# Grouped attention of a two-layer transformer step: from batch loops to one unrolled order of units with the side work between them

## Chip, cores and metric

The kernel runs on one core of one Trainium2 chip. The metric is the device time of one execution in microseconds (us), the median of several runs.

## What is computed

The inputs are 4 batches of 256 tokens with 256 features. The reference runs a cross attention with fp8 rounding, a ternary feed-forward part, a second cross attention with int8-quantised weights, and then the last layer, in which the change lies: an RMS norm, projections to 32 query heads and 8 key and value heads of 64 features, rotary parts on queries and keys, causal grouped attention (four query heads share one key head), an output projection of 2048 by 256 added to the residual stream, and a mixture of 16 experts with the four best per token. Cut to the attention of the last layer:

```python
q, k = _rope(q, k)                      # q*cos + rot(q)*sin, the same for k
# 4 query heads share a key and value head, causal
p = softmax(q @ k.T / sqrt(64) + mask)  # per batch and head, 256 x 256
x = x + (p @ v).reshape(4, 256, 2048) @ wo
```

## The kernel before, in words

Everything is one program on one core with explicit semaphores. Each engine runs its own list of instructions in the order in which the program writes them. The stages follow one another: the cross attentions and the feed-forward part (to about 338 us of the trace), the grouped attention (to about 676 us), then routing and experts. Only the grouped attention differs between the two kernels, and the names below belong to it.

**Precision.** Queries and keys are kept as two float16 halves, hi and lo. `products` multiplies hi by hi, hi by lo and lo by hi and sums in PSUM. A projection piece is 128 tokens by 512 columns: six matmuls. A batch has twelve pieces, six per block `t` of 128 tokens: the keys (`c` = 0), four pieces of queries (`c` = 1 to 4, eight heads each) and the values (`c` = 5).

**Side work of a piece** (keys and queries). TensorE projects it (`project`, products at L1648). VectorE multiplies by cosine and sine (L1323, L1324, L1326) and adds the two parts (L1330) in `rope`. ScalarE makes the hi half (`token_hi`, L885 for queries, L887 for keys; L879 is the copy of the values). GpSimd makes the lo half (`token_lo`, L696 and L698). Then TensorE turns the piece by eight transposes (`turn_tokens`, L1815), and VectorE (L1348) or ScalarE (L895) copies the turned heads from PSUM to `qt`, `kat` or `kbt`.

**Units.** A unit is one key head with its four query heads and one block of 128 queries. A batch has 16 units, alternately with 128 keys (`t` = 0) and 256 keys (`t` = 1). The chain of a unit is: scores (`a_score`, L1791 to L1793, the middle one adds the causal mask), the negated row maximum on VectorE (`score_max`, L1338), four exponentials with their sums on ScalarE (L922), reciprocal on VectorE (L1364), normalisation on GpSimd (L706), transposes on TensorE (`a_turn`, L1832), copies to `apt` by VectorE (L1360) and, for 256 keys, ScalarE (`pt_second`, L902), products with the values (`a_values`, L1847), and the hi (`output_hi`, L907) and lo (L1369) halves of the result in `ot_hi` and `ot_lo`.

**Order.** In `attend` a loop step `i` issues on TensorE the scores of unit `i`, the transposes of unit `i - 3` and the value products of unit `i - 4`. After the 16 units of a batch come the output projection (96 products of 128 by 256 in two groups, L1648), the addition to `xn` (L1382) with its statistics, and the remaining pieces of the next batch: four projections stand in steps 16 and 17, two in step 19, the other six around the output projection, the twelve turns behind them. The first three batches are one hardware loop (`Fori(0, B - 1)`) on each of the four engines, the last batch stands behind it in straight code. `turn_bank` gives each turn its PSUM bank. Scores use banks 0 to 3, transposes 4 and 5, value products 6 and 7. SyncE loads expert weights; some loads wait for the last projection (`proj`) and some for the last addition (`x4_added`). Behind the attention VectorE adds `xn` to `x`, six of eight blocks of it (L1379) ahead of the last output projection's additions.

The lines that set the order of TensorE in a batch:

```python
for i in range(AU + 4):
    if 1 <= i < AU:
        a_score(b, i)
    if 3 <= i < AU + 3:
        a_turn(i - 3)
    if i >= 4:
        a_values(i - 4)
```

## Time and profile before

| What | Value |
|---|---|
| Median of 3 runs | 863.56 us (863.39 to 863.63) |
| Profiled execution, its own time | 863.33 us |
| Its span in the trace | 861.5 us |
| Mean granted clock of TensorE, share of full | 0.9 |
| Instructions in the trace | 17134 |
| TensorE (PE) busy | 634.3 us, 74% of the span |
| VectorE (DVE) busy | 616.5 us, 72% |
| ScalarE (ACT) busy | 441.7 us, 51% |
| GpSimd (POOL) busy | 445.0 us, 52% |

How to read it: a span is the time from the first to the last instruction of the trace. The busy shares are means over stages that have different limits, so the attention is read by itself. PE is TensorE's matmuls, PEld its weight loads, which run beside them; a matmul's duration holds its passage through the array, so that neighbours overlap and the distance of starts tells the pace. Timeline rows start with the time of the first instruction and the time until the last one ends; a bracket at the end names idle time and what ended it.

### The profile page before, as it was taken

How to read it: one execution, taken by the hardware profiler on the slowest of the kernel's cores; microseconds unless marked ns; L12 is line 12 of the kernel's file. 1: busy time of each engine (PE TensorE's matmuls, PEld its weight loads, DVE VectorE, ACT ScalarE, POOL GpSimd, SP SyncE). 2: the span in 40 equal slices, each digit the busy share in tenths (PEclk: the TensorE clock that was granted, in tenths of full speed). 3: DMA queues.
4: the chain of work that ended last, by engine and by line, in shares of the span. 5: the costliest groups of instructions: out<-in, count | busy, mean ns of one | idle time of the engine just before them, and what ended most of it. 6: DMA issues, size and time to landing. Idle time of an engine off the chain costs nothing.

```text
span 861.5 us, 17134 instructions
## 1 busy us (share of the span) xinstructions
PE 634.3 (74%) x5889; PEld 462.7 (54%) x5889; DVE 616.5 (72%) x1476; ACT 441.7 (51%) x1230; POOL 445.0 (52%) x397
## 2 busy tenths in 40 slices
PE   0214997277878754589988998899798638999980
PEld 0102666255646542378666866776587515666650
DVE  5998758787887787958786777678776393555544
ACT  4712633176857711368336824773486206767650
POOL 1463763189999903435334532553264216777760
PEclk9998998698989967889999999999999758999995
DMA  9400130327656502000000000000300543333437
GB/s 291 160 1 0 50 99 21 102 75 221 206 182 198 184 37 110 1 2 2 2 1 0 0 0 0 0 0 0 146 2 2 222 160 91 108 104 107 108 88 250
DMA packets 39896, 71.73 MB, mean 83 GB/s; under 512 B 5024, under 2 KB 31392, under 8 KB 39328
## 3 DMA queue, kind: packets, MB, share of 16 engines
q1 hardware_dynamic: 35232, 58.03, 20.1%
q0 software_dynamic: 4608, 12.98, 5.1%
q8 instruction: 32, 0.52, 0.3%
q14 instruction: 24, 0.20, 0.1%
HBM read 49.96 MB, written 21.04 MB: 82 GB/s over the span
## 4 chain that ended last, share of the span: by engine, by line
PE 28%; POOL 25%; issue 23%; DVE 16%; DMA 3%; ACT 3%; SPq 1%; POOLq 0%; DVEq 0%; ACTq 0%
POOL arena L706 8%; PE ps L1940 8%; PE ps L1963 4%; PE ps L1648 3%; PE ps L1615 2%; POOL arena L661 2%; POOL arena L657 2%; PE ps L1575 2%; POOL arena L696 2%; PE ps L1593 2%; POOL work L696 2%; DVE xn L1007 1%; PE ps L1917 1%; PE ps L1847 1%; PE ps L1952 1%
## 5 line engine op out<-in xcount | busy, mean ns | idle before, releaser
L706 POOL TENSOR_TENSOR arena<-arena,tiny 128x512 f32<-128x512 f32 x64 | 93.9, 1467 | 99.1 <-DVE tiny L1364 99.1
L922 ACT ACTIVATE arena<-ps,tiny 128x128 f32<-128x128 f32 (+1 forms) x256 | 104.9, 436 | 33.4 <-DVE tiny L1338 33.4
L1338 DVE TENSOR_REDUCE tiny<-ps 128x4 f32<-128x512 f32 x64 | 61.1, 954 | 35.9 <-PE ps L1793 35.5
L1940 PE MATMUL ps<-arena 128*128 (+1 forms) x288 | 72.4, 389 | 0.8 <-issue 0.3
L1791 PE MATMUL ps<-arena 128*128 128x128 f16 (+1 forms) x256 | 61.5, 258 | 14.9 <-ACT arena L922 10.5
L1648 PE MATMUL ps<-arena,xt_hi 128*128 128x512 f16 (+1 forms) x224 | 64.4, 372 | 3.6 <-DVE xt_lo L1137 3.0
L728 POOL DMA_INDIRECT arena<-h_store,arena x48 | 47.0, 980 | 33.6 <-DVE arena L1477 19.3
L1491 DVE SCALAR_TENSOR_TENSOR ps<-ps,arena 128x256 f32<-128x256 f32 x48 | 20.8, 433 | 57.6 <-ACT arena L972 57.6
L1360 DVE COPY arena<-ps 128x512 f32<-128x512 f32 x64 | 44.0, 687 | 23.9 <-PE ps L1832 23.9
L1793 PE MATMUL ps<-arena 128*128 128x128 f16 (+1 forms) x256 | 60.4, 255 | 0.0
L734 POOL DMA_INDIRECT y_store<-arena x48 | 47.4, 988 | 21.4 <-issue 12.2
L1847 PE MATMUL ps<-arena 128*64 128x128 f32 x768 | 56.1, 281 | 2.5 <-DVE arena L1369 2.5
L1832 PE MATMUL ps<-ident,arena 128*128 128x128 f32 x384 | 54.2, 278 | 4.7 <-DVE arena L1360 2.4
L922 ACT ACTIVATION_READ_ACCUMULATOR arena<-ps,tiny 128x1 f32 x256 | 56.5, 221 | 0.0
L835 ACT ACTIVATE arena<-arena 128x256 f32<-128x256 f32 x128 | 54.6, 507 | 2.8 <-DVE arena L1250 2.6
L1792 PE MATMUL ps<-causal,ident_bf 128*128 128x128 bf16 x256 | 53.4, 227 | 0.0
L1832 PEld LDWEIGHTS ps<-ident,arena 128*128 128x128 f32 x384 | 44.0, 144 | 7.7 <-issue 6.0
L1847 PEld LDWEIGHTS ps<-arena 128*64 128x64 f32 x768 | 40.7, 136 | 13.4 <-issue 10.0
L1250 DVE CUSTOM_DVE_ANT_0 arena<-ps,arena 128x256 f32<-128x256 f32 x128 | 46.7, 420 | 0.0
L1575 PE MATMUL ps<-ident,work 128*128 128x128 f32 x64 | 14.6, 423 | 42.3 <-DVE work L1032 26.0
L1705 PE MATMUL ps<-ident,arena 128*128 128x128 f32 x256 | 36.8, 290 | 11.0 <-issue 3.3
L1648 PE MATMUL ps<-arena 128*128 128x256 f16 x384 | 43.1, 273 | 0.9 <-DVE arena L1369 0.9
(298 smaller groups left out, 1851.5 us busy)
## 6 DMA issues: line engine op xcount, KB each, us to landing
e_store<-arena SPq DMA_DIRECT2D x16, 768.0 KB, 4.3
arena<-e_store SPq DMA_DIRECT2D x16, 768.0 KB, 7.3
xn<-w_dram SPq DMA_DIRECT2D x24, 256.0 KB, 4.6
work<-w_dram SPq DMA_DIRECT2D x24, 256.0 KB, 4.7
arena<-w_gate_up_t_dram SPq DMA_DIRECT2D x2, 1024.0 KB, 9.0
arena<-wq_dram SPq DMA_DIRECT2D x2, 1024.0 KB, 7.5
arena<-wo_dram SPq DMA_DIRECT2D x2, 1024.0 KB, 5.4
work<-y_store SPq DMA_DIRECT2D x4, 512.0 KB, 6.5
```

Source lines behind the costliest of these rows:

```text
L706: nc.gpsimd.tensor_tensor(p, p, arec[:, u % 4, :].unsqueeze(2).broadcast_to([P, GH, L]), ALU.mult)\
L734: nc.gpsimd.indirect_dma_start(y_store, bass.IndirectOffsetOnAxis(index[:, i:i + 1], 0), y[:, i % YBUF, :], None).then_inc(y_sent[i % YBUF ...
L835: nc.scalar.activation(xp[:, i % 2, h, :], masked[:, i % 2, h, :], ACT.Exp, bias=xnm[:, i % 4, h:h + 1], scale=-1.0).then_inc(x_exp, 1)
L922: nc.scalar.activation(ap_[i % 3][:, h, 0:L], ps[:, (i % 2) * 2 + h // 2, (h % 2) * S:(h % 2) * S + L], ACT.Exp, bias=anm[:, i % 4, h:h + ...
L1338: nc.vector.tensor_reduce(anm[:, i % 4, :].rearrange("p (m h) -> p m h", m=2), scores, AX.X, ALU.max, negate=True).then_inc(a_max, 1)
L1648: last = mm(dst, l, r, start=(n == 0), stop=(n == 3 * len(pairs) - 1))
L1791: mm(ps[:, bank, at:at + L], q, kat[:, g, 0:L], start=True, stop=False)
L1792: mm(ps[:, bank, at + t * P:at + L], ident_bf[:, :], causal[:, :], start=False, stop=False)
L1793: last = mm(ps[:, bank, at:at + L], q, kbt[:, g, 0:L], start=False, stop=True)
L1832: last = nc.tensor.transpose(ps[:, 4 + k, h * P:(h + 1) * P], ap_[u % 3][:, h, k * P:(k + 1) * P], ident[:, :])
L1847: last = mm(ps[half * HD:(half + 1) * HD, 6 + u % 2, pair * P:(pair + 1) * P], av[:, k, g * HD:(g + 1) * HD], apt[:, u % 2, k, h * P:(h + ...
L1940: last = mm(ps[:, 2 + i % 2, :], xg[:, i % 2, x_half * KB + k, :], weights(hidden_weights(slot, w_half, k), i), start=(n == 0), stop=(n == 5))
```

## The change

The three hardware loops and the last batch's body become one unrolled loop over all 64 units (`UNITS`) on every engine, and two tables drive the side work:

- `SIDE` lists the 48 projection pieces with the unit behind which each is issued. Eight pieces of batch 0 stand in front (-1); in each batch the four query pieces of `c` = 3 and 4 of its own stand at units 0, 1, 2 and 4, and eight pieces of the next batch at units 5, 6, 8, 9, 10, 12, 13 and 14. Behind the start every piece uses PSUM bank 7.
- `TURNS` lists the 48 turns with the unit, bank and copying engine: behind the start always bank 4, ScalarE at odd units, VectorE at even ones.
- A step `i` on TensorE issues the transposes of unit `i - 2` (before `i - 3`), the scores of unit `i`, a turn and a projection where the tables have one (turn first at even units), the value products of unit `i - 2` (before `i - 4`), and six products of the output projection for unit `i - 3`. The output projection thus accumulates in bank 6 over the 16 units; both additions to `xn` and both statistics of a batch run in one go, in step 3 of the next batch.
- Scores with 128 keys use bank 0, with 256 keys banks 1 and 2. The transposes use banks 3 and 4; the value products have bank 5 alone and wait until the unit before has been read.
- The add of the rotary part moves from VectorE to GpSimd (`rope_sum`) for all pieces behind the start; there it precedes the normalisation, and the lo half follows it.
- `kat`, `kbt` and `av` are doubled (one for each parity of the batch); the halves of queries wait in a ring of four pieces (`q2`, `QRING`), the output halves in a ring of four units.
- The large addition `x + xn` runs in step 64, ahead of the last unit's copy. SyncE's list is unchanged.

The core of the diff (removed bodies and sizes of tiles are left out):

```diff
+UNITS = B * AU
+KEY, VAL = 0, 5
+def in_place_order():
+    first = [(KEY, 0), (KEY, 1), (1, 0), (1, 1), (VAL, 0), (VAL, 1), (2, 0), (2, 1)]
+    order = [(0, c, t, -1) for c, t in first]
+    own = [(3, 0), (3, 1), (4, 0), (4, 1)]
+    following = [(KEY, 0), (KEY, 1), (VAL, 0), (VAL, 1), (1, 0), (1, 1), (2, 0), (2, 1)]
+    at = [0, 1, 2, 4, 5, 6, 8, 9, 10, 12, 13, 14]
+    for b in range(B):
+        groups = [(b, c, t) for c, t in own] + [(b + 1, c, t) for c, t in following if b + 1 < B]
+        order += [g + (b * AU + u,) for g, u in zip(groups, at)]
+    return order
+SIDE_BANK = [(7, 6, 5, 2, 1, 0, 7, 6)[n] if n < 8 else 7 for n in range(len(SIDE))]
+def turns_in_order():
+    order = [(0, 0, -1, 4, "act"), (0, 1, -1, 3, "vec"), (1, 0, -1, 4, "act"), (1, 1, -1, 3, "vec"),
+             (2, 0, -1, 4, "act"), (3, 0, -1, 3, "vec")]
+    at = {(3, 0): 2, (3, 1): 3, (4, 0): 5, (4, 1): 7, (1, 0): 13, (1, 1): 14, (2, 0): 15, (2, 1): 17}
+    keys = {(0, 0): 8, (0, 1): 9, (1, 0): 10, (1, 1): 11}
...
+    return order + [(n, h, u, 4, "act" if u % 2 else "vec") for n, h, u in later]
@@ GpSimd
+            def rope_sum(n):
+                m = ROPES.index(n)
+                pool.wait_ge(rope_parts, m + 1)
+                nc.gpsimd.tensor_tensor(yb[:, m % 2, :], yb[:, m % 2, :], yr[:, m % 2, :], ALU.add).then_inc(roped, 1)
...
+            for i in range(UNITS + 1):
+                before = [n for n in sides_at(i - 1) if n in ROPES] if i else []
+                for n in before:
+                    rope_sum(n)
+                if i:
+                    normalise(i - 1)
+                for n in before:
+                    token_lo(n)
@@ ScalarE
+            for n in sides_at(-1)[:6]:
+                token_hi(n)
+            for r in turns_at(-1):
+                if TURNS[r][4] == "act":
+                    turned_tokens(r)
+            for n in sides_at(-1)[6:]:
+                token_hi(n)
+            for i in range(UNITS + 3):
+                if i >= 3:
+                    output_hi(i - 3)
+                if 2 <= i < UNITS + 2 and i % 2:
+                    pt_second(i - 2)
+                for n in sides_at(i - 1) if i else []:
+                    token_hi(n)
+                for r in turns_at(i - 1) if i else []:
+                    if TURNS[r][4] == "act":
+                        turned_tokens(r)
+                if i < UNITS:
+                    exponentials(i)
@@ VectorE
+            def add_attention(b):
+                vec.wait_ge(wo_out, (b + 1) * AU)
+                for t in range(TB):
+                    nc.vector.scalar_tensor_tensor(xn[:, b * TB + t, :], ps[:, 6, t * D:(t + 1) * D], 1.0 / WS,
+                                                   xn[:, b * TB + t, :], ALU.mult, ALU.add).then_inc(x4_added, 1)
+                vec.wait_ge(x4_added, (b + 1) * TB)
+                for t in range(TB):
+                    stat(b * TB + t, xn)
...
+            for i in range(UNITS + 3):
+                if 2 <= i < UNITS + 2:
+                    pt_first(i - 2)
+                if 1 <= i <= UNITS:
+                    row_reciprocal(i - 1)
+                if i >= 3:
+                    output_lo(i - 3)
+                if i < UNITS:
+                    score_max(i)
+                if i > AU and i % AU == 3:
+                    add_attention(i // AU - 1)
+                for r in turns_at(i):
+                    if TURNS[r][4] == "vec":
+                        turned_tokens(r)
+                for n in sides_at(i):
+                    if n in ROPES:
+                        rope(n)
+                if i == UNITS:
                     nc.vector.tensor_tensor(x[:, 0:T - TB, :], x[:, 0:T - TB, :], xn[:, 0:T - TB, :], ALU.add)
+            add_attention(B - 1)
@@ TensorE
+            def turn_tokens(r):
+                n, half, _, bank, _ = TURNS[r]
+                b, c, t, _ = SIDE[n]
+                pe.wait_ge(tok_split, ropes_to(n))
+                past = [q for q in range(r) if TURNS[q][3] == bank]
+                if past:
+                    pe.wait_ge(*read_out(past[-1]))
+                if TURNS[r][2] > 2:
+                    pe.wait_ge(a_pt2, (TURNS[r][2] - 1) // 2)
...
+            def out_projection(u):
+                b, g, t = u // AU, u % AU // TB, u % TB
+                pe.wait_ge(a_o_read, u + 1)
+                if u % AU == 0 and b:
+                    pe.wait_ge(x4_added, b * TB)
+                for o in range(2):
+                    hi, lo = ot_hi[:, u % 4, o, :], ot_lo[:, u % 4, o, :]
+                    for l, r in ((hi, wo_hi), (hi, wo_lo), (lo, wo_hi)):
...
+                        last = mm(ps[:, 6, t * D:(t + 1) * D], l, r[:, g * 2 + o, :], start=first, stop=final)
+                last.then_inc(wo_out, 1)
...
+            for n in sides_at(-1):
+                project(n)
+            pe.wait_ge(kb_zeroed, TB)
+            for r in turns_at(-1):
+                turn_tokens(r)
+            for i in range(UNITS + 3):
+                if 2 <= i < UNITS + 2:
+                    a_turn(i - 2)
+                if i < UNITS:
+                    a_score(i)
+                if i % 2 == 0:
+                    for r in turns_at(i):
+                        turn_tokens(r)
+                for n in sides_at(i):
+                    project(n)
+                if i % 2:
+                    for r in turns_at(i):
+                        turn_tokens(r)
+                if 2 <= i < UNITS + 2:
+                    a_values(i - 2)
+                if i >= 3:
+                    out_projection(i - 3)
```

## Rows read from the trace of the kernel before

**Rows 1.** Stretches: length; busy (count) of PE, PEld, DVE, ACT, POOL; PEclk; DMA.
```profile
339.57:676.26 336.69, 297.02 (x2970) 230.50 (x2968) 247.66 (x464) 188.89 (x672) 140.13 (x104) 0.95 0.03 10
...
371.26:453.43 82.17, 74.69 (x748) 58.04 (x746) 61.01 (x117) 47.02 (x168) 35.05 (x26) 0.96 0.01 1
384.95:404.59 19.64, 19.64 (x242) 16.61 (x241) 15.98 (x32) 17.26 (x77) 11.75 (x9) 1.00 0.01 2
375.00:380.00 5.00, 2.38 (x16) 1.81 (x14) 1.58 (x4) 3.33 (x16) 2.93 (x2) 0.78 0.00 2
657.23:665.15 7.92, 5.76 (x68) 4.36 (x66) 4.03 (x10) 3.74 (x12) 2.68 (x2) 1.00 0.01 2
```

**Rows 2.** Timeline of TensorE in the middle of batch 0, by starts.
```profile
394.57 0.60 PE L1832 MATMUL ps<-ident,arena 128*128 128x128 f32 x4
...
395.10 1.09 PE L1847 MATMUL ps<-arena 128*64 128x128 f32 x16
...
396.13 0.23 PE L1791 MATMUL ps<-arena 128*128 128x128 f16 x1
...
396.81 1.04 PE L1832 MATMUL ps<-ident,arena 128*128 128x128 f32 x8
...
397.78 0.66 PE L1847 MATMUL ps<-arena 128*64 128x128 f32 x8
...
398.37 0.28 PE L1791 MATMUL ps<-arena 128*128 128x256 f16 x1
...
399.48 0.60 PE L1832 MATMUL ps<-ident,arena 128*128 128x128 f32 x4
```

**Rows 3.** Waits from batch 0 to batch 1 (371.26 to 453.43 us).
```profile
POOL arena L706 <- DVE tiny L1364: 25.4, 16, 9.5
```

**Rows 4.** Timeline: two projections, the next transposes, token turns, the output projection.
```profile
413.01 0.60 PE L1648 MATMUL ps<-arena,xt_hi 128*128 128x512 f16 x2
...
415.61 0.60 PE L1832 MATMUL ps<-ident,arena 128*128 128x128 f32 x4
...
443.89 2.84 PE L1815 MATMUL ps<-ident_h,arena 128*128 128x128 f16 x48
...
665.15 10.65 PE L1648 MATMUL ps<-arena 128*128 128x256 f16 x96 [0.94 <-DVE arena L1369]
```

**Rows 5.** Timeline of one unit with 256 keys: its maximum, right behind its scores, and its normalisation.
```profile
621.02 1.23 DVE L1338 TENSOR_REDUCE tiny<-ps 128x4 f32<-128x1024 f32 x1 [1.44 <-PE ps L1793]
...
624.51 1.89 POOL L706 TENSOR_TENSOR arena<-arena,tiny 128x1024 f32<-128x1024 f32 x1 [1.06 <-DVE tiny L1364]
```

**Rows 6.** Costs of side work: batch 1's groups; by line (min/median/max), L1330 and L1379.
```profile
L1330 DVE TENSOR_TENSOR arena<-arena 128x512 f32<-128x512 f32 x10 | 9.6, 962 | 0.3
L895 ACT ACTIVATE arena<-ps 128x1024 f16<-128x1024 f16 x5 | 5.0, 1023 | 2.9 <-PE ps L1815 2.9
L696 POOL TENSOR_TENSOR arena<-arena 128x512 f16<-128x512 f32 x4 | 4.6, 1157 | 8.1 <-ACT arena L885 8.1
L885 ACT ACTIVATE arena<-arena 128x512 f16<-128x512 f32 x4 | 2.5, 630 | 8.6 <-DVE arena L1330 8.6
...
L1330 DVE TENSOR_TENSOR arena<-arena x40: 691/1145/1575, 341.0 to 610.4; 128x512 f32<-128x512 f32 x40
...
L1379 DVE TENSOR_TENSOR x<-x,xn x1: 1748/1748/1748, 665.0 to 665.0; 128x1536 f32<-128x1536 f32 x1
```

**Rows 7.** Timeline at the start and the end of the grouped attention.
```profile
339.57 0.69 DVE L1323 TENSOR_TENSOR arena<-ps,cos 128x512 f32<-128x512 f32 x1 [1.56 <-PE ps L1648]
...
364.41 2.47 DVE L1348 COPY arena<-ps 128x1024 f16<-128x1024 f16 x4
...
369.82 0.31 PE L1791 MATMUL ps<-arena 128*128 128x128 f16 x1
...
654.99 1.23 DVE L1338 TENSOR_REDUCE tiny<-ps 128x4 f32<-128x1024 f32 x1 [0.70 <-PE ps L1793]
...
675.84 0.42 DVE L1382 SCALAR_TENSOR_TENSOR xn<-ps,xn 128x256 f32<-128x256 f32 x1 [4.35 <-PE ps L1648]
```

More of the change, by code:

```diff
@@ new lines, in exponentials @@
+            def exponentials(u):
+                L = (u % TB + 1) * P
+                act.wait_ge(a_max, u + 1)
+                if u >= 3:
+                    act.wait_ge(a_pt_trans, u - 2)
+                for h in range(GH):
+                    nc.scalar.activation(ap_[u % 3][:, h, 0:L], head_scores(u, h), ACT.Exp, bias=anm[:, u % 4, h:h + 1],
+                                         accum_out=asum[:, u % 4, h:h + 1]).then_inc(a_exp, 1)
+            for n in sides_at(-1)[:6]:
+                token_hi(n)
@@ L1392, in _, with rope_whole, turned_tokens @@
-            for n in range(10):
-                rope(0, n)
-            turned_tokens(0)
-            with vec.Fori(0, B - 1) as b:
-                attend(b, True)
-            attend(B - 1, False)
+            def rope_whole(n):
+                rope(n)
+                m = ROPES.index(n)
+                vec.wait_ge(rope_parts, m + 1)
+                nc.vector.tensor_tensor(yb[:, m % 2, :], yb[:, m % 2, :], yr[:, m % 2, :], ALU.add).then_inc(roped, 1)
+            def turned_tokens(r):
+                vec.wait_ge(tok_transposed, r + 1)
+                nc.vector.tensor_copy(turn_target(r), heads_bank(TURNS[r][3])).then_inc(qt_vec, 1)
@@ L1776, in project @@
                     w = [(wq_hi[:, k, (c - 1) * 512:c * 512], wq_lo[:, k, (c - 1) * 512:c * 512]) for k in range(KB)]
-                else:
-                    w = [(wkv_hi[:, c // 5, k, :], wkv_lo[:, c // 5, k, :]) for k in range(KB)]
-                rows = bass.ds((b * TB + t) * P, P) if not isinstance(b, int) else slice((b * TB + t) * P, (b * TB + t + 1) * P)
-                products(ps[:, c, :], [((xt_hi[:, k, rows], xt_lo[:, k, rows]), w[k]) for k in range(KB)])\
+                rows = slice((b * TB + t) * P, (b * TB + t + 1) * P)
@@ L1781, in project @@
+                products(ps[:, SIDE_BANK[n], :], [((xt_hi[:, k, rows], xt_lo[:, k, rows]), w[k]) for k in range(KB)])\
                     .then_inc(proj, 1)
-            def a_score(b, u):
-                n, g, t = b * AU + u, u // TB, u % TB
+            def turn_tokens(r):
+                n, half, _, bank, _ = TURNS[r]
+                b, c, t, _ = SIDE[n]
+                pe.wait_ge(tok_split, ropes_to(n))
[4 more added lines that the diff above has]
+                    pe.wait_ge(a_pt2, (TURNS[r][2] - 1) // 2)
+                for h in range(8):
+                    src = (kb2 if half else ka)[t][:, h, :, :] if c == KEY else half_heads(n)[:, h, :, :]
+                    last = nc.tensor.transpose(ps_h[:, bank, h * P:(h + 1) * P], src.rearrange("p m d -> p (m d)"),
+                                               ident_h[:, :])
+                last.then_inc(tok_transposed, 1)
@@ L1788, in a_score @@
                 for h in range(GH):
                     q = qt[:, g * GH + h, t * P:(t + 1) * P]
[L1790 to L1793 removed]
+                    dst = head_scores(u, h)
@@ new lines, in a_values @@
+            def a_values(u):
+                b, g, t = u // AU, u % AU // TB, u % TB
+                if g == 0:
+                    pe.wait_ge(v_ready, b * TB + t + 1)
+                pe.wait_ge(a_pt, u + 1)
+                if t:
+                    pe.wait_ge(a_pt2, u // 2 + 1)
+                if u:
+                    pe.wait_ge(a_o_read, u)
+                for pair in range(GH // 2):
+                    for k in range(t + 1):
+                        for half in range(2):
+                            h = pair * 2 + half
+                            last = mm(ps[half * HD:(half + 1) * HD, 5, pair * P:(pair + 1) * P],
+                                      av[b % 2][:, k, g * HD:(g + 1) * HD], apt[:, u % 2, k, h * P:(h + 1) * P],
+                                      start=(k == 0), stop=(k == t))
+                last.then_inc(a_o, 1)
```

426 lines of the change are left out of this document (175 added, 251 removed).

## Prediction, written before the changed kernel was run

> **What bounds the kernel now.** I read the stretches of the grouped attention first: from its first rotary part to its last addition it takes 336.7 us, with TensorE busy 297.0 [rows 1]. In the middle of a batch's units TensorE is busy 19.64 of 19.64 us [rows 1], and its timeline shows a cycle without a gap: a pair of units (one with 128 keys, one with 256) is transposes 0.53, values 1.03, scores 0.68, transposes 0.97, values 0.59, scores 1.11, together 4.91 us, and the next pair's transposes start at once [rows 2]. So there TensorE is the bound, and the change removes nothing from it. VectorE (15.98) and ScalarE (17.26 of 19.64) come close behind. But a batch takes 82.2 us, not 8 x 4.91 = 39.3 [rows 1]: 42.9 us go to the passage between batches (twelve projections, the rotary parts, twelve token turns, the output projection). The waits of that stretch name its chain: GpSimd's normalisation waits 25.4 us for reciprocals in one batch [rows 3], as no unit runs in the passage.
>
> **TensorE's work per batch**, by starts. Two projections take 415.61 - 413.01 = 2.60 us, so one 1.3; 48 token transposes are six turns in 2.84, so 0.47 each; the output projection is two times 48 products in 10.65 [rows 4]. Per batch: 39.3 + 12 x 1.3 + 12 x 0.47 + 10.65 = 71.1 us. Against 82.2 that leaves 11 us per batch to win. It is the floor of the new loop, as every product remains.
>
> **The new loop.** A step i issues transposes(i-2), scores(i), a turn and/or a projection, values(i-2), output products(i-3) (six, 0.67 us). A step without side work costs 2.9 (even) or 3.35 us (odd); a projection adds 1.3, a turn 0.47. I walked one batch, every engine in its written order.
> - Round trip of an odd unit: behind its scores the maximum starts at 621.02; exponentials and reciprocal follow, and the normalisation ends at 626.40 [rows 5]: 5.4 us, 5.5 from the scores to the transposes. With side work in the following even step there are at least 5.9 us of TensorE work between, so it is hidden. Odd steps always have such a neighbour in the first three batches.
> - VectorE: the add of the rotary part (mean 0.96 us [rows 6]) leaves it. Per step it has 2.0 us of unit work on average (15.98 in eight steps [rows 1]), 1.5 of the three multiplications (2.48 per rope now, below, less the add) and in an even step at times a 0.7 copy: some 4.2, where TensorE needs 4.2 to 5.6. Hidden, just.
> - GpSimd: the add arrives there. No row has it; the nearest, a 512-wide subtraction, is 1.16 us [rows 6], with a lower bound of 0.96 (VectorE's mean) and an upper of 1.9 (the 1024-wide multiplication [rows 5]). I take 1.16. With the low halves (1.16) and a normalisation that is 4.2 us in the worst step, hidden, and it ends before the reciprocal that the normalisation needs.
> - ScalarE: a turn's copy is 1.02, a high half 0.63 [rows 6]. Here is what is not hidden. A turn in an even step waits until ScalarE has read bank 4 from the odd step before; that copy stands behind a high half and the output's high part. By my walk TensorE waits 0.8 us in steps 2 and 14, 0.5 in 10 (with 0.1 behind a value copy in 9), 1.3 in 8, where ScalarE comes late from a short step 7: **3.4 us per batch**. Bounds: nothing, or every one of the four a full 1.65 us (both copies), 6.6.
> - The attention's addition to xn (four VectorE instructions, some 1.7 us) stands in step 3 of the next batch ahead of the next copy, and output products wait for it: 0.8 us, three times. At worst all 1.7.
> - Waits added to sections on TensorE: the transposes behind fp16 work start on the beat (415.61, right behind a projection). Behind fp32 transposes about 0.09 and behind values about 0.15 is lost already (four transposes 0.53, eight 0.97), once per unit as now. I take nothing more; upper bound 0.15 for each added section.
> - Unrolling the loops: TensorE's straight prologue ran on the beat, so nothing either way.
>
> **Sum.** The region runs from the first rope, 339.57, to the end of the last addition, 675.84 + 0.42 = 676.26: 336.7 us [rows 7].
> - Start. Now ten ropes take 364.41 - 339.57 = 24.8, 2.48 each, and the first scores start 30.3 after the first rope [rows 7]. New: six ropes, the two keys dearer, 15.1; then VectorE's copy 0.6, a turn 0.9 at the lower clock, the next turn 0.8 and ScalarE's copy 1.1: first scores at 18.5. Scores 0.7, the wait for the low half of the query piece and its turn 1.6, projection 1.3, scores 1.1, projection and turn 1.8, transposes 0.5: step 2 begins its scores at **25.5**. Bounds: 23 (the copies earlier) and 29 (another rope and copy on the way).
> - 46 steps up to the last batch: 3 x (71.1 + 3.4) + 2 x 0.8 - 9.3 (steps 0 and 1, which the start holds) = **215.8**.
> - Last batch: only five steps have much side work (23.7 us with their waits). From unit 53 on nothing fills the round trip: a pair costs 5.5 + 0.97 + 1.11 and 0.1 of VectorE's queue, 7.7 us, where TensorE has work for 6.25. So 1.1 + 5 x 7.7 = 39.6. Now the drain from the last maximum to the output products takes 665.15 - 654.99 = 10.2 [rows 4, 7]; I take 10.0, then 0.7 of products and 0.85 of additions. **74.9** in all. Here the change loses: the old batch did pairs in 4.91 with a deeper queue, and paid 10.65 of products behind them.
> - Total 316.2, 20.5 less; both statistics now come behind the additions, 0.4 back: 20.1 less. The profiled execution took 863.33 us (span 861.5), 0.2 under the median of the runs, which I neglect: **843.5 us**. The tail (routing and experts) is taken as it is: the expert loads that wait for projections start sooner, the others with the last addition as now.
>
> **A rule weighed.** The rotary add is stretched while GpSimd works: fastest 691, mean 962 ns [rows 6]. VectorE's large x + xn (1.75 us [rows 6]) moves from an idle GpSimd to beside the last normalisation (1.89) and ahead of the last copy. If it must wait, the copy is some 0.7 late, which is in my 10.0; if not, the total is 0.7 less. The Trainium skill, "SBUF — State Buffer", section "Who interferes with whom", says that a VectorE instruction with two SBUF inputs contends with a GpSimd one that reads SBUF, the second blocking until the first ends. By that rule the 0.7 is right, and the trace agrees where the rotary add shows 0.96 for 0.69; the rule speaks for the other part of the change, as no other VectorE instruction of the new loop has two SBUF inputs.
>
> **Rivals.**
> - Round trips are longer than walked: 2.5 us more per batch, and 8.4 us for a pair at the end: 843.5 + 7.5 + 3.5 = 854.5. For it: four engines in fixed order, any late one passes it on. Against: TensorE has the least slack. Chance 0.2.
> - No waits: ScalarE keeps ahead (10 less), the end's pairs at 6.6 (5.5 less): 828. For it: the new step is longer by side work that is mostly TensorE's. Against: ScalarE is 88% busy in the unit pairs already [rows 1], and a copy of 1.02 with a high half comes on top in a step of 3.8. Chance 0.1.
> - Clock: in the last batch TensorE idles a fifth of each pair. Where it was half idle (2.4 of 5.0 us busy) the granted clock was 0.78, in part 1.2 and in part 2.4 GHz; where it was busy 5.8 of 7.9, it stayed 1.0 [rows 1]. Were it to fall, transposes and scores of the loop double: 2.1 x 5 = 10.5 more, 854. The Trainium skill, "TensorE: Matmul & The Clock Gate", section "HAM oscillation — how this bites in real kernels", describes such falling back between bursts; the 5.8 of 7.9 speaks against it here. Chance 0.06.
> - Slower: each section that TensorE now starts with a wait of its own costs. A unit has about 2.3 sections more (output products, sides, turns), 64 units, 147 sections. From 20.1 / 147 = 0.14 us each the gain is gone; at 0.15 they cost 22 us, 865.5. Against: the beat after fp16 work [rows 4]. Chance 0.06.
> - It does not do what it says: a buffer or bank wait serialises batches as before, little changes, 863. All four banks in question are read within a step. Chance 0.02.
>
> **Numbers.** Forecast 843.5 with chance 0.56 (own range 838 to 850). The range takes in the first and the third rival and the bounds between, and leaves out the second (828) and the last two, 0.18 together: 832 to 858. Faster than 0.2% (about what measurements of this kernel can tell, 1.7 us) 0.92, within 0.02, slower 0.06.
>
> **What would show it.** The first scores some 12 us sooner after the first rope; from one batch's step to the same of the next 75 us, TensorE busy over 90% at clock 1.0; gaps of 0.5 to 1.3 ahead of turns in steps 2, 8, 10, 14, released by ScalarE's copy; pairs of 7.7 in the last batch, TensorE waiting for GpSimd's normalisation; rotary adds near 1.16 on GpSimd. Wrong it is if a batch takes over 80 us, if the gaps stand ahead of transposes throughout, or if the tail behind the last addition is not the 185 us of now (861.5 - 676.26).

## The result, and the profile after

The changed kernel takes 847.19 us (median; 847.02 to 848.86), the kernel before in the same comparison 863.47 (862.29 to 863.63): a ratio of 0.9823, 95% interval 0.9805 to 0.9841. The forecast was 843.5 in a range of 832 to 858.

The stretches of the changed kernel (length; busy and count of PE, PEld, DVE, ACT, POOL; granted clock; DMA share, GB/s): the region from the first rotary product to the end of the last addition, one batch from a step to the same step of the next, and the last batch.
```profile
span 845.2 us, 16838 instructions
...
338.81:660.52 321.71, 290.81 (x2970) 223.07 (x2968) 209.99 (x414) 208.19 (x687) 181.62 (x138) 0.98 0.03 11
457.74:533.44 75.70, 71.45 (x747) 55.25 (x744) 49.90 (x102) 52.33 (x172) 47.28 (x37) 1.00 0.01 2
614.00:652.00 38.00, 32.34 (x356) 26.75 (x356) 20.66 (x39) 24.39 (x97) 14.63 (x10) 1.00 0.06 25
```
The region fell from 336.7 us [rows 1] to 321.7. In front of it 0.8 us went, behind it 0.5 (845.2 - 660.5 = 184.7 for 185.2): the span is 16.3 shorter and 15.0 of it are here. Of these, 8.8 are idle time of TensorE (39.7 became 30.9) and 6.2 are busy time: the same 2970 matmuls took 290.8 us for 297.0, as more of them ran at full clock (0.98 for 0.95 on average). In a batch TensorE is busy 71.45 of 75.70 us where it was 74.69 of 82.17 [rows 1], so half of the 6.5 us that a batch gained is idle time and half the clock, 1.00 for 0.96. The kernel before dropped to 0.50 (1.2 GHz) twice in the first and in the second passage between batches (from 450 to 452 and from 460 to 462 us in the first) and once in the third; between two batches of the changed kernel that no longer happens.

TensorE's waits in the region, and below them its waits from 612 us to 655 alone, in the last batch (line waited for: us in total, times, longest):
```profile
PE ps L1882 <- issue: 10.3, 9, 1.2
PE ps L1938 <- DVE arena L1448: 8.3, 11, 1.6
PE ps L1882 <- ACT arena L985: 5.8, 2, 3.0
PE ps L1882 <- DVE arena L1427: 1.9, 1, 1.9
PE ps L1954 <- DVE xn L1455: 1.8, 3, 0.6
...
PE ps L1938 <- DVE arena L1448: 6.8, 10, 1.6
```
L1882 is a token turn, L1938 the values, L1954 the output products; L985 is ScalarE's copy of a turn, L1448 VectorE's low half of an output, which reads the values' bank last, L1455 the attention's addition to xn. The first row is nine waits of 1.13 to 1.18 us ahead of the turns issued in steps 2, 8 and 14 of a batch: three from one batch's step 2 to the next one's. The profile names no releaser for them. The first batch's step 2 is not among them; its wait of 2.73 us stands in the third row, beside one of 3.0 at the start.

TensorE's timeline around two of these turns, around the first batch's step 2, and over one pair of the last batch:
```profile
397.06 0.61 PE L1882 MATMUL ps<-ident_h,arena 128*128 128x128 f16 x8 [1.18 <-issue]
426.23 0.61 PE L1882 MATMUL ps<-ident_h,arena 128*128 128x128 f16 x8 [1.13 <-issue]
...
365.10 0.66 PE L1921 MATMUL ps<-ident,arena 128*128 128x128 f32 x4 [0.43 <-POOL arena L788]
369.16 0.61 PE L1882 MATMUL ps<-ident_h,arena 128*128 128x128 f16 x8 [2.73 <-ACT arena L985]
...
635.31 0.60 PE L1921 MATMUL ps<-ident,arena 128*128 128x128 f32 x4
637.56 0.66 PE L1938 MATMUL ps<-arena 128*64 128x128 f32 x8 [0.98 <-DVE arena L1448]
638.92 1.09 PE L1921 MATMUL ps<-ident,arena 128*128 128x128 f32 x8
641.28 1.09 PE L1938 MATMUL ps<-arena 128*64 128x128 f32 x16 [0.17 <-DVE arena L1448]
642.97 0.60 PE L1921 MATMUL ps<-ident,arena 128*128 128x128 f32 x4
```
A pair of the last batch is 642.97 - 635.31 = 7.66 us, as long as forecast. But the wait in it stands ahead of the values, released by VectorE, and not ahead of the transposes (L1921), released by GpSimd, as forecast.

The first batch's step 2 took 8.49 us from scores to scores (365.59 to 374.08) where the same step of the later batches takes 5.9 (443.20 to 449.13). Only part of the 2.6 us between them is waiting: the wait is 1.6 longer (2.73 for 1.14), the step has no output products yet (0.7 less), and the granted clock of TensorE fell behind the wait, so that a projection, the values and the transposes took 1.6 us longer than at full clock:
```profile
370.04:374.08 4.04, 4.04 (x21) 2.35 (x20) 1.81 (x4) 0.76 (x4) 1.05 (x2) 0.58 0.00 0
```
Ahead of the turn, GpSimd's and ScalarE's timelines show one queue handing lateness to the other:
```profile
362.77 1.27 POOL L782 TENSOR_TENSOR arena<-arena 128x512 f32<-128x512 f32 x1 [2.73 <-DVE arena L1415]
364.00 1.04 POOL L788 TENSOR_TENSOR arena<-arena,tiny 128x512 f32<-128x512 f32 x1
365.00 1.16 POOL L776 TENSOR_TENSOR arena<-arena 128x512 f16<-128x512 f32 x1
366.12 1.26 POOL L782 TENSOR_TENSOR arena<-arena 128x512 f32<-128x512 f32 x1
...
367.47 0.63 ACT L981 ACTIVATE arena<-arena 128x512 f16<-128x512 f32 x1 [0.88 <-POOL arena L782]
368.01 1.01 ACT L985 ACTIVATE arena<-ps 128x1024 f16<-128x1024 f16 x1
```
GpSimd makes a rotary sum (L782), a normalisation (L788), a low half (L776) and the next sum with no idle time; ScalarE's high half (L981) waits for that sum, the turn's copy (L985) stands behind the high half, and TensorE's next turn waits for the copy.

### The profile page after: what moved, and what is told of

It is laid out like the page before. It is cut to its first block, busy times and chain, and to the rows that moved or that the text cites. A ratio compares the mean times of both kernels' runs of the same rounds, so it can differ in the third digit from the quotient of the medians.

```text
span 845.2 us, 16838 instructions
## 1 busy us (share of the span) xinstructions
PE 624.2 (74%) x5889; PEld 453.9 (54%) x5889; DVE 578.9 (68%) x1427; ACT 461.1 (55%) x1245; POOL 487.7 (58%) x431
## 4 chain that ended last, share of the span: by engine, by line
PE 52%; DVE 18%; POOL 13%; issue 8%; ACT 4%; DMA 3%; SPq 1%; POOLq 0%; DVEq 0%; ACTq 0%
PE ps L1737 9%; PE ps L2032 8%; PE ps L1954 5%; PE ps L1938 5%; PE ps L1921 5%; PE ps L2055 4%; PE ps L1882 2%; PE ps L1704 2%; POOL arena L743 2%; POOL arena L739 2%; PE ps L1664 2%; PE ps L1906 2%; PE ps L1904 2%; PE ps L1682 2%; DVE xn L1096 1%
## 5 line engine op out<-in xcount | busy, mean ns | idle before, releaser
L788 POOL TENSOR_TENSOR arena<-arena,tiny 128x512 f32<-128x512 f32 x64 | 93.9, 1467 | 87.4 <-DVE tiny L1444 87.4
L1938 PE MATMUL ps<-arena 128*64 128x128 f32 x768 | 56.5, 282 | 8.3 <-DVE arena L1448 8.3
L782 POOL TENSOR_TENSOR arena<-arena 128x512 f32<-128x512 f32 x34 | 43.1, 1269 | 31.3 <-DVE arena L1415 31.3
L821 POOL DMA_INDIRECT y_store<-arena x48 | 47.4, 988 | 20.5 <-issue 12.2
L1904 PE MATMUL ps<-arena 128*128 128x128 f16 (+1 forms) x256 | 58.5, 247 | 0.2 <-ACT arena L985 0.2
L1906 PE MATMUL ps<-arena 128*128 128x128 f16 (+1 forms) x256 | 58.5, 247 | 0.0
L1954 PE MATMUL ps<-arena 128*128 128x256 f16 x384 | 53.0, 274 | 2.0 <-DVE xn L1455 1.8
L1938 PEld LDWEIGHTS ps<-arena 128*64 128x64 f32 x768 | 41.2, 137 | 24.5 <-issue 12.9
L776 POOL TENSOR_TENSOR arena<-arena 128x512 f16<-128x512 f32 x36 | 41.7, 1158 | 21.2 <-ACT arena L975 11.8
L1921 PE MATMUL ps<-ident,arena 128*128 128x128 f32 x384 | 53.1, 275 | 0.4 <-POOL arena L788 0.4
L1006 ACT ACTIVATION_READ_ACCUMULATOR arena<-ps,tiny 128x1 f32 x256 | 52.1, 203 | 0.0
L1905 PE MATMUL ps<-causal,ident_bf 128*128 128x128 bf16 x256 | 51.6, 220 | 0.0
```

The lines of the kernel that those rows point to most:

```text
L788: nc.gpsimd.tensor_tensor(p, p, arec[:, u % 4, :].unsqueeze(2).broadcast_to([P, GH, L]), ALU.mult)\
L1006: nc.scalar.activation(ap_[u % 3][:, h, 0:L], head_scores(u, h), ACT.Exp, bias=anm[:, u % 4, h:h + 1], accum_out=asum[:, u % 4, h:h + 1]). ...
L1904: mm(dst, q, kat[b % 2][:, g, 0:L], start=True, stop=False)
L1905: mm(dst[:, t * P:L], ident_bf[:, :], causal[:, :], start=False, stop=False)
L1906: last = mm(dst, q, kbt[b % 2][:, g, 0:L], start=False, stop=True)
L1921: last = nc.tensor.transpose(ps[:, 3 + k, h * P:(h + 1) * P], ap_[u % 3][:, h, k * P:(k + 1) * P], ident[:, :])
```

## Experiments

Times of one group of runs were measured on one chip, against the kernel before in the same group. The region (first rotary product to end of last addition) was 321.71 and 321.55 us in the two profiles of the changed kernel, so it carries most verdicts; differences are taken from 321.55, the yardstick. In the third group (the two edits together, the output products one unit later, all three edits) every kernel was slower, the kernel before too at 899.45 us: behind the region 221.7 us passed (868.5 - 646.8) for 185 in the others, while the region's steps agree to hundredths. For that group ratios and regions are given; as the 37 us stand in both kernels, a ratio of that group understates the gain, by some 4% of it.

**The yardstick.** The changed kernel again, nothing edited.

> The changed kernel as it is, on the chip of the other runs of this group, as their yardstick. Expected: a ratio to the kernel before of 0.982 within 0.002, and a profiled span within 1.5 us of 845.2; the attention region, from the first rotary product to the end of the last addition, 321.7 us within 1.

847.47 us against 861.78, ratio 0.9825 (0.9802 to 0.9848), span 845.4, region 321.55. As expected.

**Three turns of each batch copied by VectorE.**
```diff
-    return order + [(n, h, u, 4, "act" if u % 2 else "vec") for n, h, u in later]
+    return order + [(n, h, u, 4, "act" if u % 2 and u % AU not in (1, 7, 13) else "vec") for n, h, u in later]
```


> The token turns issued in steps 2, 8 and 14 of a batch are copied by VectorE instead of ScalarE, nothing else. Theory: TensorE waits ahead of those turns (in the first batch 2.7, 1.2 and 1.1 us, in the three later ones 1.1, 1.2 and 1.1) only because ScalarE frees the bank late, behind its exponentials. Then these waits, 5.0 + 3 x 3.45 = 15.4 us less what comes up next, go: region 308 to 313 us instead of 321.7, total 834 to 839. Rival: the copy is late because of what feeds it or the turn waits for its tokens; then VectorE frees the bank no sooner and the total stays within 4 us of the changed kernel.

The turns whose copies moved are those issued in steps 1, 7 and 13; the turns in steps 2, 8 and 14, which the expectation names, are those that wait for these copies (VectorE copies them in the changed kernel already). 833.11 us, ratio to the kernel before 0.9654 (0.9631 to 0.9678), 14.4 us under the yardstick; region 306.57, 15.0 less, a little more than the theory's band (308 to 313). TensorE's waits from 360 us to 645, and a batch:
```profile
PE ps L1938 <- DVE arena L1448: 8.3, 11, 1.6
PE ps L1954 <- DVE xn L1455: 1.8, 3, 0.6
PE ps L1921 <- POOL arena L788: 1.6, 2, 1.1
...
451.43:523.19 71.76, 70.97 (x746) 55.18 (x744) 51.40 (x105) 49.08 (x169) 47.09 (x37) 1.00 0.01 2
```
Ahead of turns only 0.2 us of waiting is left (for GpSimd, in the first batch), and a batch is 71.76 us, of which TensorE is busy 70.97. So the "issue" waits were waits for ScalarE's copy. A batch lost 3.94 us with waits that sum to 3.45: each cost some 0.16 more than the profile counts as idle. In the first batch's step 2 the wait of 2.7 us became one of 1.1 for GpSimd's normalisation, and the granted clock stayed at 1.00 there. One condition more in the list of turns gives a kernel faster than both.

**The rotary sum back on VectorE.** This undoes one part of the change.
```diff
-                        rope(n)
+                        rope_whole(n)
...
-                for n in before:
-                    rope_sum(n)
```


> The rotary sum between the units goes back from GpSimd to VectorE (34 sums; the four ahead of the loop are VectorE's already), nothing else. Theory A: VectorE has room (50 of 76 us busy in a full batch), GpSimd's queue gets 1.27 us shorter per rotary part, and the first batch, where two sums stand ahead of a normalisation, gains 1 to 3 us while the later batches stay within 0.3 us each: total 1 to 4 us less. Theory B: each sum takes 1.1 us on VectorE beside a working GpSimd, stands ahead of bank reads for which TensorE waits, and costs 0.3 us or more in each of the 34 places: total 5 to 15 us more.

843.89 us, ratio 0.9781 (0.9756 to 0.9806); region 315.78, 5.8 less. By its ratio the kernel is some 3.8 us faster than the yardstick (0.9825), and the two intervals just touch; the region is clear. Theory A has the sign and the total, but not where the gain lies: two of the three "issue" waits of a batch fell by 0.6 each (their sum from 10.3 to 6.7), where it had at most 0.3 per batch. In the first batch step 2 fell from 8.50 to 6.55 us; its wait only went from 2.74 to 2.37, and the other 1.6 is the clock, which did not fall here:
```profile
366.64:373.19 6.55, 4.18 (x44) 2.96 (x42) 4.72 (x12) 4.73 (x18) 3.58 (x3) 1.00 0.00 0
```
That a slightly shorter wait kept the clock up is what the two rows side by side suggest; no run tests it by itself. Groups of VectorE (busy, mean ns) in this kernel and of GpSimd in the changed one:
```profile
L1421 DVE TENSOR_TENSOR arena<-arena 128x512 f32<-128x512 f32 x39 | 30.8, 789 | 1.3
```
```profile
L782 POOL TENSOR_TENSOR arena<-arena 128x512 f32<-128x512 f32 x34 | 43.1, 1269 | 31.3 <-DVE arena L1415 31.3
```
The same sum is 0.79 us on VectorE and 1.27 on GpSimd, and it stands ahead of ScalarE's high half. Moving it to GpSimd, which the forecast had as hidden, cost time.

**GpSimd normalises first.**
```diff
-                for n in before:
-                    rope_sum(n)
                 if i:
                     normalise(i - 1)
                 for n in before:
+                    rope_sum(n)
                     token_lo(n)
```


> GpSimd normalises a unit's weights before the rotary sum of that step instead of after it, nothing else. Theory: in the full batches the sum is done before the reciprocal is there, so order costs nothing but the sum now waits up to 2 us: ScalarE's high half, in its queue ahead of that step's exponentials, is late by as much, and steps with a rotary part get longer by 0.5 to 2 us each, total 5 to 40 us more. Rival: GpSimd's order doesn't matter, since nobody who is late waits for the sum: total within 1.5 us, or up to 2 us less where the first batch's normalisations come sooner.

915.38 us, a single run; region 389.2 (728.42 - 339.24), 67.6 more, 2.0 on average for each of the 34 sums. That is the upper end of the theory's price per part, though the steps are very unequal; its total of at most 40 was too low. Not all of it is waiting, either. The region's busy times and clock:
```profile
339.24:728.42 389.18, 311.86 (x2970) 231.88 (x2968) 212.12 (x414) 204.90 (x687) 181.63 (x138) 0.93 0.03 9
```
The same 2970 matmuls took 311.9 us for the yardstick's 290.7, at a mean clock of 0.93 for 0.98: 21 of the 67.6 us are the lower clock, which came with the longer waits, and 46 are waits. ScalarE's largest wait for the sum from 400 us to 480, here and in the yardstick, and what TensorE made of it (350 us to 720):
```profile
ACT arena L980 <- POOL arena L782: 19.5, 7, 3.2
...
PE ps L1881 <- issue: 36.2, 9, 5.1
PE ps L1937 <- DVE arena L1447: 13.0, 19, 2.1
PE ps L1881 <- ACT arena L984: 10.1, 2, 7.1
```
```profile
ACT arena L981 <- POOL arena L782: 1.2, 2, 0.6
```
What GpSimd delays, ScalarE hands on by its order: the high half stands ahead of exponentials and of the turn's copy.

**Two banks for the last values.**
```diff
-                    pe.wait_ge(a_o_read, u)
+                    pe.wait_ge(a_o_read, u if u < TWO else u - 1)
...
-ps[half * HD:(half + 1) * HD, 5, pair
+ps[half * HD:(half + 1) * HD, values_bank(u), pair
```
(TWO is 53; the bank is 5 or, for odd units from 53 on, 7.)

> The values products of the last eleven units alternate between two banks of PSUM instead of one, nothing else. Theory: the last batch's pairs of units (7.66 us each) are held by the one bank, read by VectorE before the next values may be written; then the waits ahead of the values go and a pair takes 6.3 to 6.8 us, total 4 to 7 us less. Rival (the one the prediction named): the round trip over normalisation and transposes is as long, 7.6 us; then the waits only move to the unit transposes, a pair stays above 7.4 us, and the total changes by less than 1.5 us.

848.70 us, a single run; region 322.41, 0.9 more (in its last 7.8 us the granted clock was 0.78, in the changed kernel's last 8.5 it was 1.00); a pair 7.65. The rival. TensorE's waits from 612 us to 655 (here L1928 is the unit transposes, L795 the normalisation):
```profile
PE ps L1928 <- POOL arena L795: 3.1, 5, 0.6
PE ps L1963 <- DVE arena L1455: 1.4, 4, 0.4
PE ps L1947 <- DVE arena L1447: 0.8, 1, 0.8
PE ps L1947 <- DVE arena L1455: 0.8, 1, 0.8
```
With the bank's waits gone, the normalisation's appear, and the pair is as long: two loops of the same length lie side by side.

**Thin projections.** Left out: the products of the low half of x with the high weights, in the 40 projections inside the loop.
```diff
+                    for k in range(KB):
+                        mm(ps[:, SIDE_BANK[n], :], xt_hi[:, k, rows], w[k][0], start=(k == 0), stop=False)
+                        last = mm(ps[:, SIDE_BANK[n], :], xt_hi[:, k, rows], w[k][1], start=False, stop=(k == KB - 1))
```


> The 40 projections that lie between units leave out their products of the low half of x with the high weights (so q, k and v of the last three batches have less precision); every wait, copy and turn stays. This takes 40 x 4 matmuls of 512 columns, 0.43 us per projection at half of its 0.86 for eight or some 17 us in all, from TensorE. Theory: in the three full batches TensorE is the bound (71.4 of 75.7 us busy), so 11 to 17 us come off. Rival: the period of a batch is set by the round trips between engines, and shorter projections only make longer waits ahead of turns and values: less than 6 us come off.

(The "40 x 4" is a slip: two matmuls of 0.215 us per projection, 80 in all, 17.2 us.) 836.18 us, ratio 0.9687 (0.9652 to 0.9722), 11.3 under the yardstick; region 309.99, 11.6 less. That is at the foot of the theory's 11 to 17. TensorE's waits ahead of turns grew by a third:
```profile
PE ps L1887 <- issue: 13.6, 12, 1.4
```
So TensorE's work counts, but not all of it: a step that gets shorter waits longer for ScalarE's copy.

**A deeper queue at the end.** From unit 52 on the transposes come three units behind the scores and the values four, with two banks, and the orders of TensorE and VectorE within a step are again those of the kernel before (scores ahead of transposes, the maximum first on VectorE); the output products come five units behind. The edit also gives VectorE the copy of the last turn (unit 55), which the expectation does not say.
```diff
+def due(i, shallow, deep):
+    return [u for u in (i - shallow,) if 0 <= u < DEEP] + [u for u in (i - deep,) if DEEP <= u < UNITS]
...
+                for u in due(i, 2, 4):
+                    a_values(u)
+                for u in due(i, 3, 5):
+                    out_projection(u)
```


> From unit 52 on, the distances between scores, turn, values and output products are those of the kernel before (turn three units behind the scores, values four, two banks for the values), nothing else. Theory: both round trips of the last batch (7.6 us over the normalisation, as long over the single bank, as two banks alone showed) are given more time, and a pair falls from 7.66 us to TensorE's own 6.1 to 6.5: five and a half pairs gain 6.5 to 8 us, the longer drain gives back 1 to 2, total 4 to 7 us less. Rival: ScalarE (its exponentials and copies) or GpSimd is the bound of a pair; then it stays above 7.2 us and the drain makes the total equal or up to 2 us more.

849.77 us, ratio 0.9854 (0.9837 to 0.9870); region 323.40, 1.9 more. The pair did not fall, it is 7.79 us: the rival's time, but not its reason. VectorE's and TensorE's timelines of one step (L1919 scores, L1971 output products, L1461 the low half):
```profile
628.09 1.23 DVE L1446 TENSOR_REDUCE tiny<-ps 128x4 f32<-128x1024 f32 x1 [2.02 <-PE ps L1921]
629.23 0.68 DVE L1453 COPY arena<-ps 128x512 f32<-128x512 f32 x1
629.83 0.17 DVE L1457 RECIPROCAL tiny<-tiny 128x4 f32<-128x4 f32 x1
629.91 0.40 DVE L1461 TENSOR_TENSOR arena<-ps,arena 128x256 f16<-128x256 f32 x1
...
628.42 1.09 PE L1955 MATMUL ps<-arena 128*64 128x128 f32 x16
630.37 0.83 PE L1971 MATMUL ps<-arena 128*128 128x256 f16 x6 [0.85 <-DVE arena L1461]
631.03 0.22 PE L1919 MATMUL ps<-arena 128*128 128x128 f16 x1
```
The maximum waits for TensorE's scores, copy and low half stand behind it on VectorE, and TensorE's output products wait for the low half ahead of the next scores: a third loop, made by the order of VectorE's list.

**Output products one unit later.** The same, with six for five in the last lines.
```diff
-                for u in due(i, 3, 5):
+                for u in due(i, 3, 6):
                     out_projection(u)
```


> The deep tail of the run before it (units from 52 on: turn three units behind the scores, values four, two values banks), with the output products moved one unit further back, to six behind the scores; nothing else. Theory: the deep tail gained nothing because TensorE waits ahead of the output products (0.85 and 0.59 us in each pair) for VectorE's low half, which stands behind the maximum, the copy and the reciprocal of the same step; one unit later these waits go, and a pair falls from 7.79 us to TensorE's own 6.35 to 6.6: the last scores come 5 to 7 us sooner, the longer drain gives 1 to 3 back, total 3 to 6 us less than the changed kernel. Rival: a third loop, over the maximum and ScalarE's exponentials, is nearly as long, and the pair stays above 7.2 us; then the total is that of the changed kernel within 2 us.

Ratio 0.9762 (0.9742 to 0.9782); region 315.55, 6.0 less than the yardstick and 7.9 less than the try before. The pairs are 6.18 to 6.23 us, TensorE's own time. Theory confirmed, and somewhat under its 6.35.

**The sum x + xn later.**
```diff
-                if i == UNITS:
-                    nc.vector.tensor_tensor(x[:, 0:T - TB, :], x[:, 0:T - TB, :], xn[:, 0:T - TB, :], ALU.add)
...
-            nc.vector.tensor_tensor(x[:, T - TB:T, :], x[:, T - TB:T, :], xn[:, T - TB:T, :], ALU.add)
+            nc.vector.tensor_tensor(x[:, :, :], x[:, :, :], xn[:, :, :], ALU.add)
```


> The sum of x and the attention's output over three of four row tiles is not made in step 64 but, with the last tile, after the last statistics scaling, in one instruction of 2048 elements. Theory: in step 64 it takes 3.15 us beside GpSimd's last normalisation (1.75 alone) and makes the last copies late, for which TensorE waits 1.5 us; taken out, the region ends 1.5 to 2 us sooner, and later it is hidden or costs under 0.5 us: total 1 to 2 us less. Rival: the instruction stands in front of the halves that the next projection needs and gives all back: total within 0.5 us, or up to 2 us more.

848.64 us, ratio 0.9838 (0.9824 to 0.9851); region 321.24, 0.3 less; the span 845.3 for 845.4. The rival. TensorE's waits ahead of the last two values, first in the changed kernel, then here:
```profile
652.88 0.66 PE L1938 MATMUL ps<-arena 128*64 128x128 f32 x8 [1.65 <-DVE arena L1448]
656.87 1.09 PE L1938 MATMUL ps<-arena 128*64 128x128 f32 x16 [1.54 <-DVE arena L1448]
```
```profile
652.72 0.66 PE L1936 MATMUL ps<-arena 128*64 128x128 f32 x8 [1.64 <-DVE arena L1448]
656.38 1.09 PE L1936 MATMUL ps<-arena 128*64 128x128 f32 x16 [1.21 <-DVE arena L1448]
```
Only 0.33 of the 1.54 was the sum's; most of these waits is the drain's own round trip.

**Both VectorE edits together.**

> Both earlier edits together: the turns of steps 2, 8 and 14 copied by VectorE, and the rotary sum on VectorE. Alone they took 15 and 6 us from the attention region. Theory: both shorten the same waits (ScalarE's late copy in those three steps), and with the first edit alone TensorE is busy in 71.4 of a batch's 71.8 us; so only the first batch has anything left, the region is 14 to 17 us shorter than the changed kernel's, total 830 to 833. Rival one: the gains are independent and add to 19 to 21 us, total 826 to 829. Rival two: VectorE, with ten copies and eleven sums more of 1.1 us, becomes late, and the total is above 835.

Ratio 0.9663 (0.9649 to 0.9678); region 307.12, 14.4 less than the yardstick, 0.55 more than with the copies alone. So the gains are one gain: both had shortened the wait for ScalarE's copy. By its ratio to 863.5 us it would be some 834 us, a little above the 830 to 833 expected and well above 826 to 829; the region is 14.4 less, inside the 14 to 17 expected.

**All three edits.**

> The two edits of the run before it together with the deep tail with output products six units behind. Theory: the full batches and the last batch are independent, so it gains what both do: 17 to 21 us less than the changed kernel, total 826 to 831, if the tail's pairs fall to 6.35 to 6.6 us. Rival: the tail gains nothing as in the first try, and the total is that of the two edits alone within 1.5 us.

Ratio 0.9599 (0.9582 to 0.9616), the fastest that computes the whole; region 300.88, 20.7 less than the yardstick, 6.2 less than the run before. It beats the changed kernel by 2.3% and the kernel before by 4.0%; against a kernel before of 863.5 that would be some 829 us by the ratio, or 828 by the difference of 35.3 us, worked out and not measured.

**Copies and thin projections**, with the same products left out as above.

> The turns of steps 2, 8 and 14 copied by VectorE, and the 40 projections between units without their products of the low half of x with the high weights (80 matmuls of 512 columns, 0.43 us per projection, 17.1 us in all; q, k and v of the last three batches have less precision). With the late copies in place the thin projections took 11.5 us from the attention region. Theory: what they lacked went into longer waits ahead of the turns, and once these are gone TensorE is the bound of the loop: thin projections then take 15 to 17 us more from it than the copies' edit alone, the region from the first scores to the last addition is 271 to 273 us (288.1 with the copies' edit alone), and a batch 66 us. Rival: the next round trips (maximum and exponentials, normalisation) are right behind; then less than 12 us come off and the region is 276 us or more.

818.69 us, ratio 0.9486 (0.9470 to 0.9502); region 294.34, 12.2 less than with the copies alone; from the first scores (355.95) to the last addition (631.78) 275.8. Neither theory's band holds it; the rival is nearer. TensorE's weight loads in one batch (441.04 us to 508.76) show what is right behind:
```profile
PEld ps L1926 <- POOL arena L788: 0.9, 4, 0.2
```
A batch lost 4.04 of the 5.16 us taken from it (12 x 0.43). The weight loads of the transposes now wait for the normalisation, 0.9 us in all, and one turn 0.5. A step with one projection shows it: 4.18 us (456.49 to 460.67) became 3.94 (449.60 to 453.54), 0.24 gained of 0.43. In the kernel with the copies alone TensorE is the bound, but the normalisation's loop lies only about a quarter of a us behind it in such steps.

## Why the prediction was right, and where it was off

- **Start.** First scores 18.5 us after the first rotary product (338.81 to 357.32), as forecast. Step 2's scores 26.8 after it, forecast 25.5: on the way TensorE waits 0.4 for VectorE to read a projection's bank and 0.4 for the first normalisation, neither in my walk. The other 0.5 is not told apart.
- **46 steps.** 219.8 us, forecast 215.8: 3.1 of the 4.0 us lie between step 2 of the first batch and step 2 of the second (77.6 for 74.5). Behind them the period is 75.7 for 75.3. The waits ahead of turns sum to 3.45 us per batch for 3.4: 1.14, 1.18 and 1.13 in steps 2, 8 and 14 for 0.8, 1.3 and 0.8, and none in step 10 for 0.5. That sum is nearer than its parts. ScalarE's late copy as their cause was right: with VectorE's copies they went. The attention's addition cost 0.6 for 0.8, three times.
- **The term that failed** is the wait of 0.8 in the first batch's step 2, which I took from the later ones: it was 2.73, 1.9 us more, and the clock that fell behind it cost 1.6 on top, which no term of the sum held (the first batch's step 2 has no output products yet, which gives 0.7 back). ScalarE's copy was the cause of the wait here too: with VectorE's copies 1.1 us was left, for another engine. The rotary sum on GpSimd is a small part of it, as with the sum on VectorE the wait was still 2.37. But the sum is a mis-sized term of its own: I had costed it at 1.16 and called it hidden because it ends before the reciprocal. That holds for most normalisations; yet ScalarE's high half waits for the sum. It measured 1.27, and back on VectorE it gives 5.8 us of the region, 3.6 of them from the "issue" waits, 0.4 from the wait in the first step 2 and 1.6 from the clock there.
- **Last batch.** 75.2 us, forecast 74.9, pairs of 7.66 to 7.70 for 7.7 (from one 256-key unit's scores to the next one's). The length was right, the wait was named only in half. TensorE waits for VectorE's low half of an output, which reads the single values bank last; I had not walked that loop. With a second bank the loop that I had named comes out, just as long, so that the length came right although another wait ended last is in part luck. That a deeper queue recovers the difference to TensorE's 6.25 was shown too (6.2), but only once the output products were moved as well.
- **The rule weighed.** VectorE's x + xn is 3.15 us where it was 1.75 [rows 6], from 652.64 to 655.79, beside GpSimd's normalisation from 652.28 to 654.17. This is what the Trainium skill, "SBUF — State Buffer", section "Who interferes with whom", says of such a pair of instructions, and here the trace agrees. It was worth 0.3 us and not the 0.7 in my drain.
```profile
652.64 3.15 DVE L1485 TENSOR_TENSOR x<-x,xn 128x1536 f32<-128x1536 f32 x1
...
652.28 1.89 POOL L788 TENSOR_TENSOR arena<-arena,tiny 128x1024 f32<-128x1024 f32 x1 [2.68 <-DVE tiny L1444]
```
- **Rivals.** Longer round trips: no, a batch took 75.7 and a pair 7.7. No waits: no; yet 828 is about what the kernel gives once both kinds are taken out (829 by ratio). Clock: not where I looked for it, 1.00 in the last batch with TensorE busy 32.3 of 38 us; it fell in the first batch's step 2 instead, for 1.6 us. A price per added section: no; the pairs with a deep queue run at 6.2 us with every section in them. Not doing what it says: no.

The profiled sum closes: 336.7 became 321.7 for a forecast 316.2, of which 1.3 are the start, 4.0 the 46 steps and 0.3 the last batch. The total came nearer (847.2 for 843.5) than the region (5.5 off) by luck: 0.8 us went in front of the region and 0.5 behind it, where I had nothing and 0.4 more. The edits of the experiments leave those stretches alone, and they moved by as much between runs (the region began at 336.9 to 340.5 us).

One thing the sum held without saying so: it priced every product of the batches at full clock. With the 71.1 us of work in a batch (measured 71.45) for 74.69 busy before, half of a batch's gain was the clock's. The forecast called all 11 us between 82.2 and 71.1 room to win and did not tell waiting from clock.

## What to carry to other kernels

When a stage is filled with side work between its units, TensorE's bound is only as good as the slowest bank read: look at which engine's queue frees each bank, and give the copy that is waited for to the engine with room in that step. Hidden work must be hidden from everyone who waits for it, and on an in-order engine from all who stand behind the waiter; the same 1.3 us sum was harmless to most normalisations and cost 5.8 us by way of ScalarE. A wait can cost more than its length: look at the granted clock behind it, and compare busy times of the same matmuls before calling a difference idle time. Where round trips of equal length lie side by side, relieving one shows the next and no gain: a deeper queue needs every consumer moved, the last one too.

## What the runs showed that was not expected

- How long the rotary sum of 128x512 takes on VectorE depends on what GpSimd does beside it. With the sum back on VectorE, 33 of the 40 ran beside no GpSimd instruction and took 0.69 us each, the other seven 1.06 to 1.57; in the kernel before the same holds, 16 at 0.69 and 24 at 1.14 to 1.57. So the sum was dear in the old order and is cheap in the new one. On GpSimd it took 1.27.
- Swapping two neighbouring instructions in GpSimd's order cost 68 us, 8% of the kernel, 2.0 us on average for each of 34 places; 21 of the 68 are TensorE's lower clock behind the waits.
- Waits that the profile gives to "issue" were real waits for another engine's read: moving that read took all nine away. Why one wait of the kind bears ScalarE's name and the others none stays open.
- Steps that repeat in the four batches agree to 0.01 us between batches, and between runs, while what lies behind the region took 185 us in all groups but one and some 222 in that one, in every kernel of it. The cause of that was not looked for.
